# A perceiver kernel on one core: norm vectors loaded ahead of the weights, the plan later, and the finished outputs turned in another PSUM bank

## The reference, cut to what matters

```
xn     = layer_norm(x_context, g1, b1)          # ctx rows, masked ones left out
ln_lat = layer_norm(latents, g2, b2)
q      = ln_lat @ Wq
k, v   = split(concat([xn, ln_lat]) @ Wkv)
weight = softmax(q . k / sqrt(64), masked)      # per head
out    = latents + (weight @ v) @ Wout
```

## Time and profile before

| | us |
|---|---|
| runs | 1128.66, 1128.32, 1119.39 (median 1128.32) |
| profiled execution, its own time | 1130.24 |
| its span | 1128.4, mean granted PE clock 0.962 |
| PE busy | 1037.1 (92%) |
| DVE busy | 830.5 (74%) |
| ACT busy | 648.0 (57%) |
| POOL busy | 214.4 (19%) |

### The profile page before, as it was taken

The page is one execution under the profiler, slowest core; times in us unless marked ns, Lnnn a source line. Parts: engine busy times, 40 slices in busy tenths (PEclk is TensorE's granted clock), DMA queues, the critical chain, the costliest instruction groups (busy, mean ns, idle before and its releaser), DMA issues. The chain is left out here.

```text
span 1128.4 us, 25500 instructions
## 1 busy us (share of the span) xinstructions
PE 1037.1 (92%) x8616; PEld 959.5 (85%) x8617; DVE 830.5 (74%) x3048; ACT 648.0 (57%) x1504; POOL 214.4 (19%) x259
## 2 busy tenths in 40 slices
PE   3889999999999999999999995957999999999977
PEld 3789999989999989999989994846788899889876
DVE  5777787775877686787786765567988889889642
ACT  3556566654665664555664662425676776767732
POOL 0011111110111110111111112820005203263222
PEclk9999999999999999999999997868999999999997
DMA  5000000000000000000000001600001000110001
GB/s 192 21 3 11 10 1 0 11 12 3 11 2 1 11 11 3 11 1 1 12 11 3 2 2 38 181 1 0 2 2 57 1 2 20 33 44 1 2 1 38
DMA packets 29455, 21.70 MB, mean 19 GB/s; under 512 B 13652, under 2 KB 26920, under 8 KB 29352
## 3 DMA queue, kind: packets, MB, share of 16 engines
q1 hardware_dynamic: 27824, 20.22, 6.1%
q10 hardware_dynamic: 1528, 0.14, 0.1%
HBM read 19.23 MB, written 1.05 MB: 18 GB/s over the span
## 5 line engine op out<-in xcount | busy, mean ns | idle before, releaser
L246 PEld LDWEIGHTS pv_ps<-v,pt 128*128 128x128 f32 x1792 | 214.2, 191 | 7.9 <-issue 3.2
L246 PE MATMUL pv_ps<-v,pt 128*128 128x65 f32 x1792 | 214.7, 271 | 1.6 <-DVE o L682 1.6
L660 DVE CUSTOM_DVE_ANT_0 s_sb<-s_ps,pen,mstate 128x256 f32<-128x256 f32 (+1 forms) x512 | 199.7, 445 | 17.2 <-issue 12.8
L424 ACT ACTIVATE probs<-s_sb,mbias 128x256 f32<-128x256 f32 (+1 forms) x512 | 203.2, 469 | 0.0
L554 POOL TENSOR_TENSOR o<-o,alpha 128x260 f32<-128x260 f32 x128 | 83.6, 653 | 589.8 <-ACT alpha L418 589.8
L433 ACT ACTIVATE pt<-turn 128x512 f32<-128x512 f32 x128 | 76.2, 596 | 142.3 <-PE turn L233 129.8
L233 PE MATMUL turn<-ident,probs 128*128 128x128 f32 x896 | 126.9, 283 | 3.6 <-DVE ql L638 2.1
L233 PEld LDWEIGHTS turn<-ident,probs 128*128 128x128 f32 x896 | 101.1, 147 | 13.6 <-issue 2.4
L682 DVE TENSOR_TENSOR o<-o,pv_ps 128x260 f32<-128x260 f32 x128 | 54.0, 422 | 55.1 <-PE pv_ps L246 44.2
L222 PE MATMUL s_ps<-kh,qh 64*128 64x256 f32 (+1 forms) x512 | 80.0, 308 | 10.3 <-DVE ot_lo L697 4.5
L632 DVE TENSOR_TENSOR kl<-proj,kh 128x512 fp32r<-128x512 f32 (+1 forms) x64 | 41.9, 655 | 52.5 <-ACT kh L411 51.8
(11 more groups left out here) (290 smaller groups left out, 2788.0 us busy)
## 6 DMA issues: line engine op xcount, KB each, us to landing
raw<-in_ctx SPq DMA_DIRECT2D x24, 128.0 KB, 2.1
f_wqkv_raw<-in_L_ffn_wqkv SPq DMA_DIRECT2D x6, 512.0 KB, 4.2
wkv_raw<-in_L_xattn_Wkv SPq DMA_DIRECT2D x2, 1024.0 KB, 10.5
f_w_raw<-in_L_ffn_w SPq DMA_DIRECT2D x8, 256.0 KB, 5.8
f_w_raw<-in_L_ffn_w SPq DMA_DIRECT2D x2, 640.0 KB
wq_raw<-in_L_xattn_Wq SPq DMA_DIRECT2D x1, 1024.0 KB, 7.0
wout_raw<-in_L_xattn_Wout SPq DMA_DIRECT2D x1, 1024.0 KB, 15.8
f_wo_raw<-in_L_ffn_wo SPq DMA_DIRECT2D x2, 512.0 KB, 5.2
```

What stands on the lines that cost most here:

```text
L246: last = pe.matmul(t.pv_ps[:, u, :], t.pt[g % 2][:, u, kt, :], t.v[:, kt, h, :], start=(kt == 0), stop=(kt == kts - 1))
L424: last = act.activation(t.probs[g % 2][:, u, 0:kts * P], t.s_sb[g % 2][:, u, 0:kts * P], ACT.Exp, bias=t.mbias[:, at:at + 1], scale=0.125)
L660: last = dve.tensor_tensor_reduce(out=t.s_sb[g % 2][:, u, 0:width], in0=t.s_ps[g % 2][:, u, 0:width], in1=t.pen[:, 0:width], scale=1.0, sc ...
```

## The change

- **Opening.** g2 and b2 go onto the SP queue between the first rows of x and Wq, with a semaphore of their own (gain_loaded), for which alone `gained(0, 1)` waits. The identity is now the first load on the ACT queue, and g1 and b1 the last. DVE's order is changed: the plan's comparisons come behind four weight pieces, the plan itself behind six pieces and the first keys' low part; the second keys' low part comes behind `plan_sums`. Pieces 8 and 9 move into steps 1 and 2 of the first item, the statistics of the other latents from step 1 to step 2, their normalisation from step 4 to 6, and ACT's splitting of Wout from step 2 to 4. The second key projection goes into a score bank (`key_bank`), so that it waits for nothing, and the scores of group 1 wait for it instead. PE's two small matmuls of the plan stand behind the first keys and the second query. The wait for 14 weight pieces moves from the end of the first item to step 6 of the finishing items.
- **Finishing items.** Scores are taken two groups at a time as in all other items. `turn_output` goes into bank turn1 and stands behind the projection of its step. It waits until the probabilities turned in the same step have been copied out by ACT and DVE (pt_ready). The next `turn_probs` waits until ACT has copied the quarter out (ot_stored, new). The output projection goes into turn1 too, behind the same wait. In `body` of ACT the quarter's copy moves behind the keys' and values' copies of its step.
- **Both finishing forms.** ACT copies the quarter from PSUM to a raw tile in SBUF and then makes the high part from that, two copies instead of one. DVE takes the low part from the raw tile. The last call (kind None) keeps its banks and waits for ot_stored where it waited for ot_lo to reuse them.

The core of the diff. Left out are the renamed semaphores, `bank` arguments that pass `key_bank`, `finish_bank` and `result_bank` on, and the ACT queue's reordered loads.

```diff
@@ -129,9 +127,29 @@
...
+    def load_norm(eng, which, told):
+        for part, name in enumerate("gb"):
+            with nc.allow_non_contiguous_dma("a vector of the width onto the partitions"):
+                eng.dma_start(t.norm[:, which, part * KC:(part + 1) * KC],
+                              args[f"L0_xattn_{name}{which + 1}"].rearrange("(k p) -> p k", p=P)).then_inc(s[told], 16)
+    def key_bank(m, u):
+        opening = isinstance(m, int) and m == 0 and u == 1
+        return t.s_ps[1][:, 0:2, :].rearrange("p u n -> p (u n)") if opening else t.proj[:]
     def query_bank(u, first):
...
         return t.turn[u % 2] if first else (t.turn[1], t.turn[1], t.proj, t.turn[1])[u]
+    def finish_bank(kind, u):
+        return t.turn[1][:] if kind else t.s_ps[FINISH_BUFFER[u]][:, 0:2, :].rearrange("p u n -> p (u n)")
+    def result_bank(kind, qt):
+        return t.turn[1][:, qt * D:(qt + 1) * D] if kind else t.s_ps[1 - qt][:, 0, :]
@@ -148,11 +166,12 @@
...
             sp.dma_start(t.x[:, 0:QT, :], rows[:, 0:QT, :]).then_inc(s["first_x_loaded"], 16)
+            load_norm(sp, 1, "gain_loaded")
             sp.dma_start(t.wq_raw[:], args["L0_xattn_Wq"].rearrange("(k p) n -> p k n", p=P)).then_inc(s["wq_loaded"], 16)
...
             sp.dma_start(t.wkv_raw[:, :, value_cols], wkv[:, :, value_cols]).then_inc(s["wv_loaded"], 16)
-            sp.dma_start(t.x[:, QT:TILES, :], rows[:, QT:TILES, :]).then_inc(s["x_loaded"], 16)
-            sp.dma_start(t.wout_raw[:], args["L0_xattn_Wout"].rearrange("(k p) n -> p k n", p=P)).then_inc(s["wout_loaded"], 16)
+            sp.dma_start(t.x[:, QT:TILES, :], rows[:, QT:TILES, :]).then_inc(s["rest_loaded"], 16)
+            sp.dma_start(t.wout_raw[:], args["L0_xattn_Wout"].rearrange("(k p) n -> p k n", p=P)).then_inc(s["rest_loaded"], 16)
@@ -215,6 +234,8 @@
...
                     pe.wait_ge(s["k_ready"], 4 * m + g // 2 + 1)
+                elif isinstance(m, int) and g == 1:
+                    pe.wait_ge(s["k_ready"], 2)
                 pe.wait_ge(s["s_read"], 8 * m + g + 1)
@@ -317,44 +338,48 @@
...
                             pe.wait_ge(s["q_ready"], 4 * b + j // 2 + 1)
-                        if finish and j in (2, 3, 5, 6):
-                            pe.wait_ge(s["ot_lo"], 4 * b - 4 + {2: 1, 3: 2, 5: 3, 6: 4}[j])
-                        if finish and j == 7:
-                            pe.wait_ge(s["x_added"], 2 * b + 1)
-                        if kind == "pair" and j == 0:
-                            pe.wait_ge(s["x_added"], 2 * b + 2)
-                        for g in [j] if finish else [j, j + 1] if j % 2 == 0 else []:
+                        for g in [j, j + 1] if j % 2 == 0 else []:
                             scores(m, g, KINDS[kind])
...
                     now = at_step(m, kind, prev, j - 2)
+                    if finish and kind and j in (2, 3, 5, 6):
+                        pe.wait_ge(s["ot_stored"], 4 * b - 4 + {2: 1, 3: 2, 5: 3, 6: 4}[j])
+                    if finish and kind and j == 7:
+                        pe.wait_ge(s["x_added"], 2 * b + 1)
+                    if kind == "pair" and j == 0:
+                        pe.wait_ge(s["x_added"], 2 * b + 2)
                     if now:
                         turn_probs(*now)
-                    if finish and j in (1, 2, 4, 5):
-                        u = {1: 0, 2: 1, 4: 2, 5: 3}[j]
+                    u = {1: 0, 2: 1, 4: 2, 5: 3}.get(j)
+                    if kind is None and u is not None:
                         if u % 2 == 0:
                             pe.wait_ge(s["o_norm"], 2 * b - 2 + u // 2 + 1)
-                        if kind:
-                            pe.wait_ge(s["s_read"], 8 * m + j + 2)
-                        elif u >= 2:
-                            pe.wait_ge(s["ot_lo"], 4 * b - 2)
-                        turn_output(b, u)
-                    if finish and j == 6:
+                        if u >= 2:
+                            pe.wait_ge(s["ot_stored"], 4 * b - 2)
+                        turn_output(b, u, kind)
+                    if kind is None and j == 6:
                         pe.wait_ge(s["ot_lo"], 4 * b)
-                        if kind:
-                            pe.wait_ge(s["s_read"], 8 * m + 8)
-                        output_projection(b, 0)
-                        if kind is None:
-                            output_projection(b, 1)
-                    if finish and j == 7:
-                        pe.wait_ge(s["s_read"], 8 * m + 9)
-                        output_projection(b, 1)
+                        for qt in range(QT):
+                            output_projection(b, qt, kind)
                     if kind:
...
                         query(0, 2 + j, True)
+                    if finish and kind and (u is not None or j >= 6):
+                        turned_m, turned_g, _ = now
+                        pe.wait_ge(s["pt_ready"], 16 * turned_m + 2 * turned_g + 2)
+                        if u is not None and u % 2 == 0:
+                            pe.wait_ge(s["o_norm"], 2 * b - 2 + u // 2 + 1)
+                        if u is not None:
+                            turn_output(b, u, kind)
+                        if j == 6:
+                            pe.wait_ge(s["w_lo"], 14)
+                            pe.wait_ge(s["ot_lo"], 4 * b)
+                        if j >= 6:
+                            output_projection(b, j - 6, kind)
                     now = at_step(m, kind, prev, j - 3)
@@ -367,26 +392,24 @@
...
-            def output_weights():
-                pe.wait_ge(s["w_lo"], 14)
             pe.wait_ge(s["ident_loaded"], 16)
             turn_tokens(0)
+            pe.wait_ge(s["x_ready"], 1)
+            pe.wait_ge(s["w_lo"], 1)
+            query(0, 0, True)
+            pe.wait_ge(s["w_lo"], 2)
+            project_keys(0, KB)
             pe.wait_ge(s["flags_ready"], 2)
-            pe.matmul(t.pv_ps[:, 0, 0:1], t.below[:].rearrange("p b c -> p (b c)"), t.listed[:, NCH:NCH + 1], start=True, stop=True).then_inc(s["flags_ranked"], 1)
-            pe.wait_ge(s["x_ready"], 1)
-            for u in range(2):
-                pe.wait_ge(s["w_lo"], 2 * u + 1)
-                query(0, u, True)
-                if u == 0:
-                    pe.wait_ge(s["keys_spread"], 1)
-                    pe.matmul(t.pv_ps[0:B, 1, 0:NCH + 1], t.row_of[:], t.listed[:], start=True, stop=True).then_inc(s["keys_listed"], 1)
-                pe.wait_ge(s["w_lo"], 2 * u + 2)
-                if u:
-                    pe.wait_ge(s["k_ready"], 1)
-                project_keys(u, KB)
+            pe.matmul(t.pv_ps[:, 0, 0:1], t.below[:].rearrange("p b c -> p (b c)"), t.listed[:, NCH:NCH + 1], start=True, stop=True
+                      ).then_inc(s["flags_ranked"], 1)
+            pe.wait_ge(s["w_lo"], 3)
+            query(0, 1, True)
+            pe.wait_ge(s["keys_spread"], 1)
+            pe.matmul(t.pv_ps[0:B, 1, 0:NCH + 1], t.row_of[:], t.listed[:], start=True, stop=True).then_inc(s["keys_listed"], 1)
+            pe.wait_ge(s["w_lo"], 4)
+            project_keys(1, KB, key_bank(0, 1))
             pe.wait_ge(s["plan_rows"], 1)
-            walk(pe, body, output_weights)
+            walk(pe, body)
@@ -437,10 +460,12 @@
...
-            def store_output(b, u):
+            def store_output(b, u, kind):
                 act.wait_ge(s["o_turned"], 4 * b - 4 + u + 1)
-                act.activation(t.ot[0][:, 2 * u:2 * u + 2, :].rearrange("p k n -> p (k n)"),
-                               t.s_ps[FINISH_BUFFER[u]][:, 0:2, :].rearrange("p u n -> p (u n)"), ACT.Copy).then_inc(s["ot_hi"], 1)
+                raw = t.ot_raw[:, 2 * u:2 * u + 2, :].rearrange("p k n -> p (k n)")
+                act.activation(raw, finish_bank(kind, u), ACT.Copy).then_inc(s["ot_stored"], 1)
+                act.wait_ge(s["ot_stored"], 4 * b - 4 + u + 1)
+                act.activation(t.ot[0][:, 2 * u:2 * u + 2, :].rearrange("p k n -> p (k n)"), raw, ACT.Copy).then_inc(s["ot_hi"], 1)
@@ -481,13 +507,15 @@
...
                                 query_hi(b + 1, 1, False)
+                        if u is not None:
+                            store_output(b, u, kind)
                         if prev is not None or j != 1:
...
                             query_hi(0, 2 + j, True)
-                        if prev is None and j == 2:
+                        if prev is None and j == 4:
                             first_deviations(slice(QT, TILES), 2)
-                            act.wait_ge(s["wout_loaded"], 16)
+                            act.wait_ge(s["rest_loaded"], 32)
                             weights_hi(range(10, 14))
@@ -694,13 +715,13 @@
...
                 out, hi = (o[:, 2 * u:2 * u + 2, :].rearrange("p k n -> p (k n)") for o in (t.ot[1], t.ot[0]))
-                dve.tensor_tensor(out, t.s_ps[FINISH_BUFFER[u]][:, 0:2, :].rearrange("p u n -> p (u n)"), hi.bitcast(F32),
-                                  ALU.subtract).then_inc(s["ot_lo"], 1)
```

(27 more changed lines are left out.)

55 lines of the change are left out of this document (24 added, 31 removed).

## The result

Medians of five runs each: 1128.32 us before (1119.39 to 1128.83), 1136.49 us after (1129.06 to 1136.65); ratio 1.0081 (95% interval 1.0046 to 1.0116). A second set of four runs gave 1135.88, ratio 1.0105 (1.0066 to 1.0144). The change costs about 1%: the interval leaves out 1, but 8 us is less than the 11.3 us that the prediction took as the bound of what can be told. Forecast were 1133 us, a range of 1119 to 1141, and a difference within 1%. Of the ten executions of the kernel before in the last group of runs one took 3449.9 us, three times the others, and the ratios leave it out.

The account below looks back on a forecast made before the run. PE, busy 92% of the span, was taken as the bound. Opening -2.0, three finishing items +6.0 and last call +1.0 gave +5.0 us: 1133 us against the median, own range 1127 to 1139, 8 in 10 within 1119 to 1141.

Parts of the forecast that it names:

- The main step: Finishing items: DVE copies turn1 1.0 us late and stands ahead of output_lo; 6.8 us of waits against 4.1.
- step 4: Finishing item: DVE has 4.0 us of work between two copies; PE waits 1.6 us.
- step 5: Finishing item: DVE needs 6.3 us from copy to copy, PE's own work is 4.4; PE waits 1.9 us.
- the chain: Finishing item carried through step by step from 230.77: end at 281.95 instead of 280.40, +1.55 us.
- The first product's step: Opening: weights delayed 0.5 us (bounds 0 to 1.0), first product at 15.1, 2.6 us earlier than 17.73.
- The plan's wait: Opening: PE waits 1.5 us for DVE's plan ahead of any scores, which start at 25.5.
- the lead of 1.2 us: Opening: next projection starts at 29.7 instead of 30.87; 1.2 us won, carried to the first item's end.
- Last call: ACT's path behind the last quarters is 2 x 0.57 longer and exposed: +1.0 us, bounds 0.6 and 2.
- A: Rival: the clock falls once in each finishing item and once in the opening; 1140 us, chance 0.15.
- B: Rival: DVE runs ahead enough, turn1 is free, clock never falls; 3.5 us won an item, 1116 us, chance 0.13.
- C: Rival: waits of about the old size in new places, items at 0, opening -3, end +1; 1126 us, chance 0.22.
- D: Rival: the plan's DMA in the opening comes back 3 us later, opening gives +1; 1136 us, chance 0.05.

Follow-up runs that it names:

- the raw copy in the score banks: Against the opening alone: ACT's raw copy added, next scores wait for it, turned quarters stay in the score banks; 1113.12 us, ratio 0.9882.
- the low part one step later: Changed kernel with DVE's low part of a turned quarter made one step later; one run, 1124.97 us.
- the wait put back: The opening alone with PE's wait for the 14th weight piece again ahead of the loop; one run, 1121.16 us.
- the repeat: The changed kernel once more with nothing changed; 1135.88 us, four runs.
- the opening alone: Changed kernel's opening with the finishing items of before and no raw copies; 1118.85 us, ratio 0.994 to the kernel before.
- finishing items alone: Changed kernel's finishing items and last call with the opening of before; 1142.1 us, ratio 1.0155 to the kernel before.

## Why the prediction was right, and where its terms were off

**The main step held.** It said that turn1 is the wrong bank, because DVE copies it 1.0 us after PE is done with the projection, and that DVE would stand ahead of `output_lo` for ACT's second copy. Both are there. The waits in PE's order, forecast and measured: keys 1.0 and 1.16; step 2, 0.95 and 0.48; step 4, 1.6 and 1.03; step 5, 1.9 and 1.39; step 6, up to 0.3 and 0.36; step 7, 1.0 and 0.94. With 0.27 for the sum in step 3 that nobody forecast, the waits are 5.6 us, 1.2 less than the 6.8 that I had.

**The item came out at +3.1, not +2.0,** and the term that was mis-sized is PE's busy time. Forecast was +4.4 of idle time, -1.7 for the clock and -0.6 for scores in pairs. Measured is +4.1 of idle time (6.5 against 2.4) and, with the 1.7 of clock gone as forecast, +0.7 of busy time where I had -0.6.

The idle time came out near because two errors met: the waits above are 1.2 us less, and the 0.7 us for x at the item's end, counted as saved, went but left 0.58 us of the loop's own start in its place. The busy time is another matter. Scores in pairs save what I said (four pairs of 1.62 us instead of 1.80, 0.7 us; elsewhere the prediction had priced the same thing below 0.1 for each of four). Yet PE is busy 46.26 us against 45.52 in the form with single scores and full clock. A quarter behind a wait takes 0.50 us to the next instruction instead of 0.35, and the probabilities of step 4 take longer, as PE's timeline of the kernel after shows:

```profile
249.53 1.09 PE L254 MATMUL turn<-ident,probs 128*128 128x128 f32 x8
250.77 0.39 PE L63 MATMUL proj<-xt_hi,wkv_hi 128*128 128x256 f32 x1
```

From one start to the other are 1.24 us, where the raw copy in the score banks has 0.93 (248.84 to 249.77). Short holds of this kind count as busy, and I had given them nothing. They go with DVE's standing like the long waits: with the low part one step later the same stretch is 1.00 us, and PE's busy time in the item falls by 1.0. Of my two figures, +1.55 by the chain and +2.1 by the terms, both were too small.

**The opening came out at -3.3, not -2.0,** and of its parts some missed by more than the sum shows.

The first product's step had the right chain and a wrong size: key weights at ACT plus 1.7, 0.6 and 0.7 gives 16.4 from 13.41, and 16.38 was measured; the delay of the weights was 1.77 us instead of 0.5, outside the bounds of 0 to 1.0. The nearest row could not price it, because no load of such vectors stood ahead of weights on one queue. The Trainium skill, DMA: Bandwidth & Descriptors, section Rules for kernel authors, says that a strided last dimension becomes one descriptor per element, and that is how these vectors are loaded. By it I had put the delay at 1.0, nearer than my own figure. The traces agree in kind: from 3 to 7 us the queue that carries the weights moved 748 packets and 0.39 MB, where it had moved 407 and 1.02 MB before. The size, 1.77 us, is theirs alone.

The plan's wait was 0.81 instead of 1.5, because PE came to it 1.5 us later than forecast (25.5 instead of 24.0) and the plan only 0.9 later (26.27 instead of 25.4). The second keys' wait was 2.23 instead of 2.4. The clock did fall behind it, as the prediction allowed at a price of 1.7, but for twice as long as the stretch that this price was read from: 0.52 over 7 us, up to 3.4 us lost. The item's next scores start at 39.1 instead of 36.97.

So the lead of 1.2 us that I carried to the end of the first item was not there: PE's last work in it ends 1.2 us later than before. What made up for it is the loop's start. I gave it a pause of 2.7 us because PE had begun 2.7 us behind the last piece; it is 0.62 us without a wait. The 2.5 to 2.7 us stand only where PE waits for the piece, as the wait put back shows, and are not a cost of the loop itself. At the first pair item the forecast of -2.0 met -2.30, and that is luck: the item was 2.4 us worse than I had it, and the pause 2.1 us better.

Half clock behind the 4.13 us pause is gone too. The clock was 0.69 from 75.09 to 80 us before and is 1.00 from 72.79 to 80 after, and with it the lead grows from 2.30 to 3.33 us.

**Last call** +0.7 instead of +1.0, and this is luck as well. The path itself grew by 1.6 us, 0.67 ahead of the second `onorm` and 0.96 in the wait that I had priced; I had left out the first. The shorter stretch at half clock behind it took back 0.93.

**Sum.** -3.3 + 9.4 + 0.7 = +6.8 against +5.0; two errors, -1.3 and +3.4, partly offset each other. The direction and the main cost are the prediction's own; that the number is so near is in part luck.

**Rivals.** A (the clock falls in the finishing items) did not come: clock 1.00 in all three and again in the repeat, behind waits of 1.16, 1.03 and 1.39 us. Its fall in the opening did come. Its time, 1140, was near the one measured all the same, since the items are longer for another reason. B (all waits but those for keys gone) is what happens with the score banks kept: 3.2 us an item won, in another kernel than the one forecast. C (items at 0) and D (the plan's DMA late) are out: the plan's sums begin at 28.09 behind a plan that ended at 26.27, 1.8 us, no more than the 2.0 of before.

**What stays open:** why PE needs 2.5 us behind a release ahead of the loop; how much of the rest of the item's +3.1, beyond the two thirds above, is the late copy of turn1 itself; and where the last 1.4 us of the medians' difference lie, since the later stages alone differ by 8 us between two executions.

## What to carry to other kernels

Before moving work into a bank, look at when its slowest reader is done in a normal step, and release a contested bank by the shortest copy that frees it; splitting the copy was worth 3.2 us an item (1.5 where the clock had not fallen), and moving the bank cost 3.1. A gain measured over a piece of a loop has to be checked over the whole period, since the engine that runs late carries its debt into the next piece. And before a gain in a trace is given to an edit, the granted clock of the stretches in which it arises has to be compared: 1.4 of the 5.2 us of the opening alone were the clock's. Small loads of single numbers go on a queue on which nothing large is waited for.

## What the runs showed of the hardware

- Two vectors, 512 numbers of 4 bytes, ahead of a load of weights on its queue held it to 15 and 35 GB/s for two microseconds, and the next weights came 1.8 us later (13.41 to 14.05 us in eight executions). With the vectors on the other queue the weights came at 11.65 and 12.21 us, as without them (11.64 and 12.29).
- The same wait of 1.49 to 1.50 us at the same place is followed by half clock in some executions and not in others. In windows of the opening alone, where the scores behind it end:

```profile
237.80:241.40 3.60, 3.60 (x18) 3.31 (x17) 3.35 (x15) 1.31 (x3) 0.00 (x0) 0.58 0.02 5
```

and in windows of the kernel with the wait for 14 pieces, behind the 1.49 us at 244.17:

```profile
234.04:282.01 47.97, 45.61 (x398) 42.21 (x398) 36.39 (x139) 26.62 (x64) 5.29 (x8) 1.00 0.03 7
244.00:250.00 6.00, 5.83 (x53) 5.23 (x54) 5.17 (x19) 4.25 (x12) 1.01 (x2) 1.00 0.01 3
```

The item is 49.58 us in the one and 47.97 in the other, 1.6 us apart. Both happen within one execution too: in the second finishing item of the kernel with the wait for 14 pieces the clock is 0.59 from 408 to 411 us, behind the same 1.49 us (at 406.83).
- Behind a wait of 2.11 us at one place of the first item the clock was low for some 3 us in one execution (0.58 from 40 to 44 us, kernel before) and for some 10 us in another (0.56 from 41 to 52 us, finishing items alone).
- PE starts 2.5 to 2.7 us behind a semaphore it waits for ahead of the loop (three executions), and 0.6 us behind its own last work where nothing is waited for.
